# A three-layer field-interaction tower on one core: two vector steps moved by one chunk, the last product cut in four, and twenty matmuls on a buffer of ones at the start

## The reference

```python
e = stack([tbl_f[ids[:, f]] for f in range(39)], axis=1)          # 512 x 39 x 16
prev = e
for k in range(3):
    z = einsum('bmd,bhd->bdmh', e, prev).reshape(b, D, m * h)
    t = einsum('bdc,co->bdo', z, ws[k]) + bs[k]                   # 128 units
    t = transpose(t, (0, 2, 1))
    t = t / sqrt(sum(t * t, axis=(-2, -1), keepdims=True))
    logit.append(t)
    prev = t
z = sum(concatenate(logit, axis=1), axis=-1)                      # 512 x 384
h = relu(concatenate([z, dense_ctx], axis=1) @ W_top1 + b_top1)   # 400 -> 512
h = relu(h @ W_top2 + b_top2)                                     # 512 -> 256
y = h @ W_top3                                                    # 256 -> 1
```

## Time and profile before

| | |
|---|---|
| time, median of 3 runs | 1162.03 us (1161.07 to 1164.78) |
| the profiled execution's own time | 1161.5 us |
| its span in the trace | 1159.7 us |
| PE busy (matmuls) | 1114.0 us, 96% |
| DVE busy | 994.6 us, 86% |
| POOL busy | 945.2 us, 82% |
| ACT busy | 144.3 us, 12% |

### The profile page before, as it was taken

How to read it: one execution, slowest core, us unless ns; L and a number is a source line. 1 busy time by engine, 2 the same in 40 slices (tenths; PEclk the granted TensorE clock), 3 DMA queues, 4 the chain that set the end, 5 groups by cost and what they waited for, 6 DMA issues and landing times. The chain is left out here.

```text
span 1159.7 us, 22367 instructions
## 1 busy us (share of the span) xinstructions
PE 1114.0 (96%) x8252; PEld 608.7 (52%) x8252; DVE 994.6 (86%) x875; ACT 144.3 (12%) x298; POOL 945.2 (82%) x646
## 2 busy tenths in 40 slices
PE   0799999999999999999999999999999999999989
PEld 0255555555555555555555555555555555555543
DVE  2689989898998989899898989989898998989782
ACT  0010111111011110101111010111101011110102
POOL 4579888897988889798888979888898988957680
PEclk9899999999999999999999999999999999999999
DMA  7869366372936637293662728366282845727010
GB/s 239 265 223 317 97 229 200 110 258 63 319 104 222 204 102 262 65 313 112 213 214 94 267 67 310 116 210 217 86 275 68 300 126 200 225 73 283 1 52 1
DMA packets 103177, 205.81 MB, mean 177 GB/s; under 512 B 49915, under 2 KB 56251, under 8 KB 103158
## 3 DMA queue, kind: packets, MB, share of 16 engines
q1 hardware_dynamic: 94468, 203.89, 52.4%
q0 software_dynamic: 5120, 1.29, 1.3%
q10 hardware_dynamic: 3570, 0.37, 0.2%
HBM read 203.05 MB, written 2.46 MB: 177 GB/s over the span
## 5 line engine op out<-in xcount | busy, mean ns | idle before, releaser
L648 DVE TENSOR_TENSOR z<-t_ps,xb 128x2048 f32<-128x2048 f32 (+2 forms) x352 | 711.0, 2043 | 67.8 <-PE acc L825 45.1
L356 POOL TENSOR_TENSOR sums<-z,sums 128x1024 f32<-128x1024 f32 x224 | 531.0, 2370 | 53.7 <-DVE sums L661 38.5
L825 PE MATMUL mix_ps<-sums,s_sb 128*64 128x256 f32 x1792 | 330.6, 380 | 2.9 <-POOL sums L356 1.7
L811 PE MATMUL acc<-z,w_sb 128*64 128x512 f32 x1408 | 323.6, 595 | 6.7 <-DVE z L648 6.7
L353 POOL TENSOR_TENSOR sums<-z 128x512 f32<-128x512 f32 x192 | 245.4, 1278 | 69.2 <-DVE z L648 65.3
L825 PE MATMUL acc<-z,w_sb 128*64 128x256 f32 x896 | 268.1, 381 | 0.5 <-DVE z L648 0.3
L825 PE MATMUL mix_ps<-z,w_sb 128*64 128x256 f32 x896 | 268.1, 381 | 0.0
L825 PE MATMUL acc<-z,s_sb 128*64 128x256 f32 x896 | 267.0, 380 | 0.0
L825 PE MATMUL p_ps<-z,w_sb 128*64 128x256 f32 x896 | 267.0, 380 | 0.0
L825 PEld LDWEIGHTS mix_ps<-sums,s_sb 128*64 128x64 f32 x1792 | 187.0, 137 | 100.7 <-POOL sums L356 14.1
L825 PE MATMUL acc<-sums,w_sb 128*64 128x256 f32 x896 | 230.9, 380 | 0.0
(11 more groups left out here) (80 smaller groups left out, 446.8 us busy)
## 6 DMA issues: line engine op xcount, KB each, us to landing
xb<-xt SPq DMA_DIRECT2D x128, 512.0 KB, 6.7
xb<-xq SPq DMA_DIRECT2D x112, 512.0 KB, 5.1
xb<-xt SPq DMA_DIRECT2D x48, 768.0 KB, 6.7
xr<-xt SPq DMA_DIRECT2D x48, 468.0 KB
w_sb<-in_w SPq DMA_DIRECT2D x2, 2496.0 KB, 19.9
xr<-xt SPq DMA_DIRECT2D x16, 234.0 KB
x<-xt SPq DMA_DIRECT2D x15, 234.0 KB
gathered<-in_table,rows_of POOLq DMA_INDIRECT x160, 2.9
```

The lines of the kernel that those rows point to most:

```text
L356: nc.gpsimd.tensor_tensor(t41, b2, t2_twice, ALU.subtract).then_inc(t41_ready, 1)
L648: nc.vector.tensor_tensor(z[:, at:at + n, :], t_ps[k - 1][:, :].rearrange("p (a n) -> p a n", a=1).broadcast_to([P, n, N]), xb[:, XB_ROW[c ...
L811: last = nc.tensor.matmul(acc[k][o, :], w_sb[k][:, field + r, o], z[:, at + r, :], start=(c == 0 and r == 0), stop=(c == NCH - 1 and r == ...
L825: return nc.tensor.matmul(bank[side, cols], weights, moving, start=start, stop=stop, skip_group_check=True)
```

## The change

It has four parts.

1. `shared_sums(i - 1, 2)` comes one chunk earlier in DVE's program: after the products of c1 of layer 1, ahead of those of c2.
2. `normalize` is cut in two. Its four steps to the inverse norm stay after c8 of layer 2. The features (now `features`) and `scale0` come after the products of c9.
3. The last product (256 to 1) is cut into four matmuls of 128 columns for each block of inputs, with the output rows at partitions 0, 32, 64 and 96. ACT copies 128 partitions x 128 columns in place of 1 x 512, and SP's write takes four rows of 128.
4. DVE fills the buffer `cross` with ones as its first operation, and PE runs twenty matmuls of 128 x 128 x 512 on it into `mix_ps` before its wait for the first operands. Nothing reads their result.

```diff
@@
+WARM = 20
+Y_AT = 32
@@
-        y_sb = traw0[0:1, :]
+        y_sb = traw0[:, 0:P]
@@ sync
-            sp.dma_start(out.rearrange("b a -> a b"), y_sb).then_inc(y_written, 16)
+            sp.dma_start(out.rearrange("(g n) a -> g (n a)", n=P),
+                         traw0[0:P:Y_AT, 0:P]).then_inc(y_written, 16)
@@ scalar
-            nc.scalar.copy(y_sb, nrm_ps[0:1, :]).then_inc(y_ready, 1)
+            nc.scalar.copy(y_sb, nrm_ps[:, 0:P]).then_inc(y_ready, 1)
@@ vector
-            def normalize(event, k0, k1, dsum=dsum):
-                if k0 == 0:
-                    dve.wait_ge(dsum_ready, 1 if at_first(event) else 3 * event)
-                else:
-                    dve.wait_ge(dsum_ready, LAYERS * TILES - (2 - k0))
+            def normalize(event, k0, k1):
...
+            def features(event, k0, k1, dsum=dsum):
+                if k0 == 0:
+                    dve.wait_ge(dsum_ready, 1 if at_first(event) else 3 * event)
+                else:
+                    dve.wait_ge(dsum_ready, LAYERS * TILES - (2 - k0))
                 dve.wait_ge(norm_step, 4 * event + 4)
@@ tile, layer 1
-                    if c == 2 and not first:
+                    if c == 1 and not first:
                         shared_sums(i - 1, 2)
@@ tile, layer 2
                     if c == 8:
                         normalize(i + 1, *layers_of(first, last))
+                    if c == 9:
+                        features(i + 1, *layers_of(first, last))
                         if not last:
                             scale0(i + 1)
@@ start of the vector program
+            nc.vector.memset(cross[:, :], 1.0).then_inc(filled, 1)
@@ tensor
+            pe.wait_ge(filled, 1)
+            for _ in range(WARM):
+                nc.tensor.matmul(mix_ps[:, :], cross[:, 0:UNITS], cross[:, :], start=True, stop=True)
             pe.wait_ge(w0_ready, 1)
@@ end of the tensor program
-                last = nc.tensor.matmul(nrm_ps[0:1, :], wt3_sb[:, k:k + 1], h2[:, k, :],
-                                        start=(k == 0), stop=(k == TOP2 // P - 1))
+                for g in range(BATCH // P):
+                    last = nc.tensor.matmul(nrm_ps[g * Y_AT:g * Y_AT + 1, 0:P], wt3_sb[:, k:k + 1],
+                                            h2[:, k, g * P:(g + 1) * P],
+                                            start=(k == 0), stop=(k == TOP2 // P - 1))
```

More of the change, by code:

```diff
@@ L214, in build @@
         s_step = [None, sem("s1_step"), sem("s2_step")]
-        ones_ready, pads_ready = sem("ones_ready"), sem("pads_ready")
+        ones_ready, pads_ready, filled = sem("ones_ready"), sem("pads_ready"), sem("filled")
         x3_loaded, x3_copied = sem("x3_loaded"), sem("x3_copied")
@@ L779, in _ @@
             sum_d(0, 0, dsum_alone)
-            normalize(0, 0, 1, dsum_alone)
+            normalize(0, 0, 1)
+            features(0, 0, 1, dsum_alone)
             scale0(0)
@@ L789, in _ @@
             sum_d(2, TILES - 1, dsum_alone)
-            normalize(TILES + 1, 2, 3, dsum_alone)
+            normalize(TILES + 1, 2, 3)
+            features(TILES + 1, 2, 3, dsum_alone)
         @block.tensor
```

## The result

The change takes **1154.09 us** (median of 4 runs, 1153.53 to 1158.06), the kernel before 1161.55 in the same comparison (4 runs, 1160.84 to 1164.78): a ratio of 0.994, 95% interval 0.9915 to 0.9966. It is faster by 7.5 us where 4.9 were forecast, inside the range. The profiled execution is the longest of the four, 1158.06 (span 1156.3), and so it was again in x5, 1158.07: what these two traces show in the first tile need not be in the other executions.

What follows compares the result with a forecast made beforehand. PE was taken to bound the loop, so only its waits could go: 4.0 us from the loop plus 0.9 from the end, 4.9 off 1161.5, gave 1156.6, or 1157.1 as median; range 1153.5 to 1161.0.

Steps and rivals of the forecast that it cites:

- Wait A: PE waits for POOL's sums in c9 of layer 2, about 0.27 us in tiles 1 to 14; forecast to go.
- wait B: PE waits for DVE's shared sums before c1 of layer 1, about 0.22 us at all 15 turns; forecast to go.
- Wait C: New wait forecast for PE at POOL's sums in c6 of layer 1: 0.20 to 0.32 us, taken as 0.22 per tile.
- the chain comes 0.07 to 0.19 us earlier, PE 0.49 earlier: Step giving Wait C: DVE, ACT and POOL's chain to c6's sums in layer 1 gains less than PE does.
- the end: Last product, copy and write: 0.6 us off PE, 0.3 off the copy, write unchanged; 0.9 together, bounds 0.1 and 1.15.
- no new wait: Rival: the chain to c6 is shorter than held, so the loop gives 7.1 us: 1154.0; chance 0.10.
- its own range: Range of the forecast alone, without rivals: 1155.5 to 1158.8 us, for Wait C from 0.32 to 0.15 and the end's bounds.
- The twenty matmuls: At the start: end at about 21.6 us, PE idles 9.7, layer 0 still starts at 1.2 GHz; worth 0.
- The clock holds over the idle 9.7 us: Rival: layer 0 then runs at 2.4 GHz, 2.3 us more gained: 1154.8; chance 0.07.
- They touch nothing that anyone waits for: Claim that the twenty matmuls on ones, run while PE is idle at the start, cost nothing.
- The waiting for ACT: DVE's first shared sum, at its new place ahead of c2, waits 0.2 us for ACT's copy.
- the rival: DVE stands for ACT at the new place: copy 0.9 us later gives 1170.6; decides from about 0.3 over; chance 0.05.

Runs made afterwards that it cites:

- x5: The change once more, unaltered, for more runs and a second trace: 1153.42 us (5 runs), ratio 0.9932 to the kernel before.
- x6: Kernel before with only the shared sums one chunk earlier; no ones, last product as before: 1160.21 us (12 runs), ratio 0.999.
- x7: Kernel before with only features and `scale0` moved behind c9; no ones, last product as before: 1157.97 us (9 runs), ratio 0.9975.
- x8: The change with 31 matmuls on ones in place of 20, up to the first operands: 1156.7 us (5 runs), ratio 0.9963.
- x2: Kernel before with only the twenty matmuls on ones and the fill added: 1163.39 us (12 runs), ratio 1.0015.
- x10: x2 with the twenty written-out matmuls on one column in place of 512: 1162.82 us (12 runs), ratio 1.0014.
- x3: Kernel before with only the last product in four quarters, its copy and write of four rows: 1160.92 us (12 runs), ratio 0.9995.
- x4: The change without its twenty matmuls on ones and without the fill: 1153.03 us (6 runs), ratio 0.9926.
- x9: x2 with the twenty matmuls as a loop on PE in place of written out: 1162.04 us (12 runs), ratio 1.0009.
- x11: x4 with, in tile 0, all of DVE's layer 0 products for tile 1 made behind c10: 1153.28 us (6 runs), ratio 0.9929.
- x12: x11 with POOL's memset of the pads in the last tile behind c8's sums: 1153.09 us (6 runs), ratio 0.9925.

## Why the prediction was right, and where it was off

**Wait A and wait B, 7.1 us: right.** Place, releaser and size of both held, and x6 and x7 show each going with its own move, but for 0.06 us that x6 gives back in A. The loop gave 7.4 us.

**Wait C, 0.22 us a tile: this step failed.** The step said "the chain comes 0.07 to 0.19 us earlier, PE 0.49 earlier". The first number was 0.46. I had followed DVE's own queue from the sums to c5 and stopped there, as if what stood behind were fixed. In fact 0.24 had been won at ACT's copy behind c5, a little more than forecast, 0.09 more at DVE's sum, and 0.13 more inside two products, where the times fit a DVE that had been held up by PE itself. With 0.22 x 15 = 3.3 us that term is more than the whole miss of 2.6 (7.5 measured, 4.9 forecast); the end took 0.5 of it back, and the rest is within what the runs can tell. The rival "no new wait", given 0.10, is what happened. Its 1154.0 is the median to 0.1, and that is luck: it started from 1162.0 where the kernel before had 1161.55 here, and took 0.9 for the end where 0.37 came. The forecast itself holds the time only because its range was opened to that rival: its own range, 1155.5 to 1158.8, does not reach 1154.09. (By the terms that it names, that range should read 1155.8 to 1159.4, that is 1162.0 - 15 x (0.49 - 0.15) - 1.15 and 1162.0 - 15 x (0.49 - 0.32) - 0.1.) The reserve left, 0.04 over the signal, says how near C was.

**The last product, 0.9 us: 0.37.** PE gave 1.08 - 0.40 = 0.68 (0.6 forecast), the copy 0.30 (0.3 forecast), and the write cost 1.70 - 1.15 = 0.55 where 0, and 0.2 either way, was taken, and 0.06 was lost in the steps between. The write's bounds were too narrow: no row showed such a write. On the weight loads the trace decides against the page: by the Trainium skill, page "TensorE: Matmul & The Clock Gate", section "Part 3: Packing small matmuls — row/col tiling", a weight load overlaps matmuls in flight only when it is for other rows, and here eight records of loads for the same rows take 0.10 us in all from 1153.39, where the first matmul starts, and the four quarters run side by side in 0.40.

**The twenty matmuls, 0: right as to the gain.** They ended at 21.87 (forecast 21.6), PE idled 9.66 us (9.7) and layer 0 started at 1.2 GHz. "The clock holds over the idle 9.7 us" is refuted by the windows; x8, where the clock held into layer 0, was not faster but slower. "They touch nothing that anyone waits for" is not shown: x2 and x10 lie on the slower side of the kernel before.

**The waiting for ACT: 0.41 us, twice the 0.2 counted.** That is 0.21 over the estimate, and the prediction had the rival decide from about 0.3 over. It cost nothing here, since the links behind it came earlier all the same.

## What to carry to other kernels

When a wait is removed, follow the chain to the next tight place on both sides, wait by wait: a chain that is itself held up by the engine you speed up comes earlier with it, and a reserve of 0.16 us need not turn into a wait. Work that fills an engine's idle start won nothing here, even where it sped up the first layer; look at what the first tile waits for before warming anything. Cutting a result into rows to shorten the product gave back 0.55 of 0.98 us in the write. And time the loop by its tiles: a gain of 2 us in the loop can hide behind a first tile that differs by as much from one execution to the next.

## What the runs showed that was not expected

- Four rows of 512 bytes from four partitions: 0.64 us of issue and 1.70 to the wait's end, against 0.25 and 1.15 for one row of 2048 bytes.
- Four matmuls of one output row each, all 128 rows, 128 columns: 0.40 us for eight records, loads within 0.10 us.
- Layer 0 ended at another point in each execution: from 39.63 to 42.37 us in the eight traces without ones (x3 and the kernel before; x4 40.56), from 39.57 to 41.05 in the four with twenty full ones (x5 and x9; the change 39.78), and at 38.84 with 31. The medians do not follow it.
- The granted clock in the windows cannot be used at the start: it reads 1.00 over the first records of layer 0 in the kernel before (31.30 to 35.50), though the loads are 0.86 us apart as late as 39.13. The distance of the loads tells it.
- Near 80 us, behind a wait of PE at c10 of layer 1, the grant fell to 0.50 for 3 to 7 us in five of the fourteen traces: the change, x5, x2, x8, and x6, which has no ones (waits of 2.60 to 3.89 us). In these the first turn came at 121.50 to 124.22 us, in the other nine at 118.54 to 120.31.
- With the ones written out on 512 columns, each of the four traces has DVE's first product on the load `xr` of tile 1 at 73.7 to 74.5 us; with no ones (x11 and x12 aside, whose program puts it behind c10), with the same work in a loop, or with the same code on one column it began at 70.8 to 72.8.
